# ScalarE's queue issues five of the twelve transfers that fill the first element's attention stacks

## What is computed

```python
h = _ln(x) * (1.0 + scale_msa[:, None, :]) + shift_msa[:, None, :]
qkv = (h @ w_qkv).reshape(B, N, 3, HEADS, hd)
...
attn = jax.nn.softmax(jnp.einsum('bhqd,bhkd->bhqk', q, k) * scale, axis=-1)
o = jnp.einsum('bhqk,bhkd->bhqd', attn, v).transpose(0, 2, 1, 3).reshape(B, N, D)
o = o @ w_proj + b_proj
x = x + gate_msa[:, None, :] * o
```

## Time and profile before

| what | value |
|---|---|
| median of 3 runs | 458.74 us (458.56 to 458.84) |
| the profiled execution's own time | 458.03 us |
| its span | 456.3 us |
| TensorE busy | 303.2 us (66%) |
| VectorE busy | 307.5 us (67%) |
| ScalarE busy | 240.1 us (53%) |
| GpSimd busy | 133.7 us (29%) |
| mean granted TensorE clock | 0.84 of full speed |

### The profile page before, as it was taken

How to read it: one execution, slowest core, us unless ns; L and a number is a source line. 1 busy time by engine, 2 the same in 40 slices (tenths; PEclk the granted TensorE clock), 3 DMA queues, 4 the chain that set the end, 5 groups by cost and what they waited for, 6 DMA issues and landing times.

```text
span 456.3 us, 5838 instructions
## 1 busy us (share of the span) xinstructions
PE 303.2 (66%) x1953; PEld 148.0 (32%) x1954; DVE 307.5 (67%) x791; ACT 240.1 (53%) x422; POOL 133.7 (29%) x237
## 2 busy tenths in 40 slices
PE   0012862642055647699999987885777899889686
PEld 0001821431022432122222222554443444344254
DVE  0688788776858865999999950433568678766330
ACT  2276926555166421267777777433342456665742
POOL 0013102232236240253223004218340344444520
PEclk9999985555555576679999999999796599999999
DMA  7960044000000033200000000000037000000001
GB/s 240 414 260 0 1 92 94 0 0 0 0 1 1 0 96 102 79 5 1 3 3 2 3 2 1 0 1 0 0 84 195 3 5 2 3 3 5 2 0 46
DMA packets 12138, 19.96 MB, mean 44 GB/s; under 512 B 2598, under 2 KB 11050, under 8 KB 11434
## 3 DMA queue, kind: packets, MB, share of 16 engines
q1 hardware_dynamic: 12108, 19.59, 13.7%
HBM read 12.51 MB, written 0.52 MB: 29 GB/s over the span
## 4 chain that ended last, share of the span: by engine, by line
PE 38%; DVE 30%; ACT 11%; POOL 7%; issue 6%; DMA 3%; SPq 2%; DVEq 0%; ACTq 0%; POOLq 0%
DVE nm L961 10%; PE ps L1483 8%; PE ps L1469 6%; PE pe L1395 4%; PE ps L1551 4%; PE pe L1506 3%; POOL rstd L344 2%; PE ps L1442 2%; ACT scr L1079 2%; DMA big<-nmp 2%; DVE st L539 2%; SPq L324 1%; DMA big<-in_wa 1%; DVE xn L549 1%; PE ps L1266 1%
## 5 line engine op out<-in xcount | busy, mean ns | idle before, releaser
L961 DVE TENSOR_REDUCE nm<-ps 128x1 f32<-128x512 f32 (+2 forms) x224 | 131.8, 647 | 21.6 <-PE ps L1469 20.4
L1192 ACT ACTIVATE scr<-pe 128x1024 f32<-128x1024 f32 (+3 forms) x128 | 105.6, 867 | 66.0 <-PE pe L1506 65.0
L1469 PE MATMUL ps<-big 64*128 64x512 bf16 (+3 forms) x256 | 71.4, 381 | 6.9 <-DVE nm L961 4.5
L1483 PE MATMUL ps<-scr 128*32 128x512 f32 (+3 forms) x512 | 58.8, 531 | 6.3 <-ACT scr L1167 4.8
L344 POOL TENSOR_TENSOR rstd<-var,half 128x4 f32<-128x4 f32 x26 | 28.5, 1097 | 102.7 <-DVE var L544 77.2
L1506 PE MATMUL pe<-big 64*128 64x512 bf16 (+3 forms) x256 | 44.0, 355 | 3.4 <-ACT scr L1192 2.0
L1469 PEld LDWEIGHTS ps<-big 64*128 64x128 bf16 x256 | 21.0, 101 | 54.1 <-DVE nm L961 44.3
L450 POOL TENSOR_SCALAR_AFFINE_SELECT scr<-scr 128x256 f32<-128x256 f32 x64 | 25.8, 407 | 37.7 <-ACT scr L1192 36.4
L438 POOL CAST nm<-nm 128x16 bf16<-128x16 f32 x16 | 3.1, 196 | 87.2 <-DVE nm L961 87.2
L1466 PE MATMUL ps<-cmask 64*128 64x128 bf16 (+1 forms) x192 | 25.7, 261 | 3.3 <-DMA big<-tern 2.8
L549 DVE TENSOR_SCALAR xn<-x_tok,mv,rstd 128x128 f32<-128x128 f32 x60 | 17.1, 348 | 15.8 <-POOL rstd L344 15.8
(11 more groups left out here) (222 smaller groups left out, 584.1 us busy)
## 6 DMA issues: line engine op xcount, KB each, us to landing
big<-tern SPq DMA_DIRECT2D x48, 128.0 KB, 2.4
big<-in_wa SPq DMA_DIRECT2D x1, 2304.0 KB, 12.7
w<-in_w SPq DMA_DIRECT2D x2, 1152.0 KB, 19.5
big<-in_wa SPq DMA_DIRECT2D x1, 1344.0 KB, 6.4
big<-in_w SPq DMA_DIRECT2D x1, 1024.0 KB, 14.6
w<-in_w SPq DMA_DIRECT2D x1, 896.0 KB, 20.2
rowg<-in_rowg SPq DMA_DIRECT2D x1, 832.0 KB, 18.6
row<-in_row SPq DMA_DIRECT2D x1, 640.0 KB, 14.8
```

The lines of the kernel that those rows point to most:

```text
L961: v.tensor_reduce(dst, src[:, 0:w * len(hs)].rearrange("p (h w) -> p h w", w=w), AX.X, ALU.max, negate=True).then_inc(sem(f"a{a}_max"), 1)
L1192: s_.activation(P[:, kt % 2, 2 * p:2 * p + 2, q0:S], E[(e - 1) % 2][:, :, q0:S], ACT.Exp, scale=SCALE).then_inc(sem(f"a{a}_p"), 1)
L1469: last = t_.matmul(dst[:, k * wd:(k + 1) * wd], stack_of(a, 0, b, HG * g + h, qt * 128, (qt + 1) * 128), stack_of(a, 1, b, HG * g + h, 0, ...
L1483: last = t_.matmul(bank[6][32 * h:32 * h + 32, q0:S], V[b][:, kt, HG * g + h, :], P[:, kt % 2, h, q0:S], start=(kt == 0), stop=(kt == TB - 1),
```

## The change

For element 0 of each attention layer the five transfers of the keys' high and middle pieces are taken out of SP's list and put into ScalarE's: three right after ScalarE has made the high pieces, two right after the middle ones. ScalarE waits there for its own semaphore (`hi`, then `mid`, both at 2) before it issues. SP skips both the waits and the transfers. The number of transfers, their sizes, their places and the count of `stack0` stay.

```diff
                 for b in range(B):
                     for part, made in enumerate(("hi", "mid", "split")):
                         for qk, pieces in enumerate((PIECES, PIECES_K)):
+                            if (b, qk) == (0, 1) and part < 2:
+                                continue
                             sp.wait_ge(sem(f"a{a}_{made}"), 2 * b + qk + 1)
...
             for n, kind, layer in SEQ:
                 if kind == "att":
                     a, causal = (0, False) if layer == 1 else (1, True)
+
+                    def keys_to_stack(part):
+
+                        act.wait_ge(sem(f"a{a}_" + ("hi", "mid")[part]), 2)
+                        for j in [j for j, piece in enumerate(PIECES_K) if piece == part]:
+                            act.dma_start(stacks[PLACE[j]::8, a, 1, 0], spl[:, 1, part, 0, :]).then_inc(
+                                sem(f"a{a}_stack0"), 16)
+
                     for b in range(B):
                         modulate(n, b, bank[TURN_BANK], "n_T", TURNS.index((n, b)) + 1)
                         for qk in range(2):
                             i = 2 * b + qk
                             act.wait_ge(sem(f"a{a}_qk"), i + 1)
                             s_.copy(spl[:, qk, 0, b], bank[QK_BANKS[i]]).then_inc(sem(f"a{a}_hi"), 1)
+                        if b == 0:
+                            keys_to_stack(0)
                         for qk in range(2):
                             i = 2 * b + qk
                             act.wait_ge(sem(f"a{a}_r"), i + 1)
                             s_.copy(spl[:, qk, 1, b], resid[:, qk]).then_inc(sem(f"a{a}_mid"), 1)
+                        if b == 0:
+                            keys_to_stack(1)
```

## The result

The changed kernel took 464.7 us at the median of four executions (463.38 to 466.53), the kernel before 458.78. The ratio on record is 1.011, with a 95% interval of 1.0065 to 1.0156: slower by 5.0 us, and by 3.0 to 7.2 within the interval. (The two medians are 5.9 us apart. Both kernels scatter more than the first few executions showed: 35 executions of the kernel before on the chip of the second set lay between 457.45 and 463.43, with a median of 460.2.

What follows compares the result with a forecast made beforehand. No engine alone bounds the kernel: L1's chain runs through ScalarE and VectorE; in L3 the stack's transfers and element 1's pieces end almost together. 1.8 + 2.2 = 4.0 us on 458.74 gave 462.7 us, range 459.9 to 465.8.

Steps and rivals of the forecast that it cites:

- The forecast's own spread, 461.5 to 463.9: Total time if TensorE's clock added 0.9 us in L3 or saved 0.9 us in L1.
- rival A: Both layers: issues of SP's and ScalarE's queues wait for each other, adding 2.6 us, 465.3 us in all; chance 0.18.
- d: Time for which one DMA issue holds ScalarE's list, taken as 0.64 us from SP's rows; range nothing to 1.28.
- B: Rival, both layers: an issue is cheaper on ScalarE, 0.29 us, costing 1.1 us together, 459.9 us in all; chance 0.10.
- C: Rival, both layers: an issue hardly holds ScalarE, up to about 0.15 us; 459 us in all; chance 0.07.
- D: Rival, L3: issues cost near nothing, the stack fills earlier and TensorE's clock stays up; faster, 457.0 us; chance 0.05.
- L1, three issues, +1.8: In L1 the issues after the high pieces delay ScalarE's middle pieces and VectorE's residual, costing 1.8 us.
- L3, 2.38 late, 2.2 net: In L3 ScalarE's issues start element 1's `hT` 2.38 us late; less VectorE's idle time, the cost is 2.2 us.
- The credit of 0.2: In L3, VectorE's idle time between 345.8 and 354.1, 0.25 us, goes away; taken as 0.2 us gained.
- The sum, 4.0: Loss over both layers: 1.8 us in L1 plus 2.2 us in L3, with the queues issuing side by side.
- The clock: TensorE's low clock on element 1's products: +0.9 us in L3, -0.9 us in L1, both taken as spread.
- a sign of being wrong: A shift of over 1 us made by the clock in stretches that the change doesn't touch.

Runs made afterwards that it cites:

- the second set: The change run again, unaltered, against the kernel before on another chip: eleven executions, ten in the ratio, 464.58 us at the median, ratio 1.0093.
- fitted fillers: Matmuls nobody reads, cut to TensorE's waits: ten in L1, four in L3 of the change, ratio 1.003; eight in L1 of the kernel before, ratio 0.9949.

## Why the prediction was right, and what it missed

The measured time, 464.7 us, lies in the range of 459.9 to 465.8, and the mechanism was the one forecast. There is luck in it all the same. The forecast's own spread, 461.5 to 463.9, leaves 464.7 out, and the range holds it only because its upper end was set by rival A, which the traces refute. As a loss it is nearer: 4.3 to 5.0 by the two ratios, against a spread of 2.8 to 5.2. The starting point of 458.74 was also three close executions of a kernel whose median over 35 is 460.2.

- **d, the time of an issue on ScalarE.** Taken as 0.64 from SP's rows; it measured 0.62 at the median, and 1.91 us for three. An issue that holds ScalarE for that long leaves nothing of rivals B, C and D.
- **L1, three issues, +1.8.** It was +1.83, and the two behind the middle pieces cost nothing, as the kernel with the middle pieces alone shows.
- **L3, 2.38 late, 2.2 net.** The modulation was 2.28 late. The working let the pair of middle pieces hold ScalarE for its whole 1.22 us, but from its start to the next instruction it is 339.32 - 338.19 = 1.13 in the forecast's own rows; that is the 0.1 too many. The credit of 0.2 behind it was 0.15 in the profiled execution (11.63 against 11.78). That the stack's wait would disappear was right, and the chain went over ScalarE to the first maximum.
- **The sum, 4.0.** From the traces it is 1.83 + 2.28 - 0.15 = 3.96, and with the clock held by fillers in both kernels the difference is 3.7. This part stood.
- **The clock.** Here the forecast fell short. It took the clock as a spread to either side, +0.9 in L3 and -0.9 in L1. In L3 the products were 1.3 (7.92) and 1.6 us (8.20) longer in the two traces of the change, and 1.3 to 1.6 in each of the three other kernels without fillers where `hT` was late, so it is a cost and no coin toss; the fitted fillers took it away. In L1 the saving never came, and no cost is shown either: the kernels with a later turn there took 13.10, 11.66, 12.95 and 11.73, those with L1 as before 11.60, 13.07, 12.37 and 12.36. So the two clock terms don't cancel, as the sum had them. The one in L3 was also mis-sized: I priced one product at the low clock (2.07 against 1.13), and the stretch holds two and the values. With it the sum is 4.0 + 1.3 = 5.3, above the 4.3 to 5.0 of the two sets and inside both their intervals.
- **Rival A, the shared descriptor generator.** ScalarE's issues lasted 671 ns at most, not 1.2 us, though they fell beside SP's third high q. The longest of SP's took 801, where the usual one takes 600. The Trainium skill's page "Perfetto Trace Analysis", section "DMA Instruction — HWDGE (DVE, Sync)", says that the generator is locked for exclusive use while it is set up and makes the descriptors. If two issues waited for each other here, it was for no more than these 0.07 and 0.2 us. What the two queues do share shows in the landings of the same 128 KB. In L1 SP's transfers took 2.4 us from issue to landing in the kernel before, one like the other; in the change SP's seven for element 0 took 2.4 to 4.1 with a median of 3.5, and ScalarE's five 2.7 to 3.6 with a median of 3.3. The page "DMA: Bandwidth & Descriptors" of the Trainium skill, section "Issuing engines are not separate DMA queues", says that DMAs of either issuer run on the same 16 DMA engines and interleave, and the rows agree.
- **The profiled execution** grew by 7.6 us in its span: 1.83 and 2.28 of hold, 1.50 and 1.29 in the two product stretches, and the last 0.7 in stretches that the change doesn't touch. The 1.50 is not shown to be the change's either, since L1's products scatter that far without it. The 0.7 is a net sum: from L1's copy of the values to L3's first modulation it took 1.1 us more (188.91 to 337.86 against 185.95 to 333.77). That is just over the 1 us that the forecast named as a sign of being wrong if the clock made it; what made it wasn't followed up. The execution was slower than the median of its kernel by 1 us.

What stays open: what sets the scatter of 6 us of the kernel before between executions. The L1 products at 11.60 to 13.07 us in kernels whose L1 is that of before point to the clock for a part of it, and so do the clocks on record: of the 91 executions on the three chips the 15 with a mean granted clock of 0.83 or less took 462.3 to 463.5 us, the other 76 took 457.4 to 462.1. But with fitted fillers, which hold the clock in L1's products in the profiled execution, the kernel before still scatters by 5.1 us (455.9 to 461.0). So most of it lies elsewhere or in executions that no trace shows, and no run was made to follow it.

## What to carry to other kernels

Moving one of these DMA issues to ScalarE cost ScalarE's list 0.6 us each time, whatever the chain said of the queue it left. Price such a move by what stands behind the issue, and put it where the engine waits for something else (here 7.5 us wide in L1, free of charge). Where a chain runs through one queue, look for a second leg that ends in the same tenth of a microsecond before shortening the first. And a delay ahead of a short burst on TensorE costs twice when the granted clock falls in it. Filling a wait with products that nobody reads, fitted so that they end ahead of it, gained 0.5% here; moving two transfers to a better place gained 0.4% in one set and nothing in the next.

## What I had not expected

The clock's cost in L3 came in full for a hold of 1.37 us as for one of 2.28 (7.99 and 7.92 to 8.20). TensorE's idle time ahead of the products was 3.25 and 4.16 us in these, and 1.87 in the kernel before, where no such cost shows (6.63): between the values tried it looks like a step and not a slope. And holding the clock at 2.4 GHz through L3's first maxima, until 354 us, gained 0.1 us, where keeping it for L1's products gained 1.5: the same clock is worth what the engine behind it waits for.
